# Rows of queries and keys with the heads next to each other, stacked by three DMAs of 256 KB for twelve of 64 KB

## The chip, the cores and the metric

The kernel runs on one core of a Trainium2 chip. The metric is the device time of one execution in microseconds. TensorE (PE) multiplies, VectorE (DVE), ScalarE (ACT) and GpSimd (POOL) work element by element, SyncE (SP) issues most DMAs. Each engine executes its own queue in order, and they meet at semaphores.

## The reference

Eight images of 512 tokens by 512 features go through an attention layer and a quantized feed-forward layer, each followed by an addition and a normalisation:

```python
q = (x @ Wq)  # 16 heads of 32;  k, v = x @ Wk, x @ Wv  # 4 heads, each for 4 query heads
attn = softmax(q k^T / sqrt(32));  x = layernorm(x + (attn v) @ Wo)
w_q = int8(round(weight / w_scale));  x_q = int8(round(x / x_scale))   # per row
x = layernorm(x + (x_q @ w_q^T) * x_scale * w_scale + bias)
```

## The kernel before

**Split numbers.** Matrix products are made from operands split in a high part (float32r) and a low part. A projection (`front_job`, L344, matmuls at L341) takes 12 matmuls of 128 x 512: four slices of the features, each high times high, high times low and low times high. Its result is 128 rows by 512 tokens: four heads of 32 rows, one below the other. ACT casts it to the high part (L657), DVE subtracts to get the low part (L843), into `q_parts` or `k_parts`.

**Stacks.** Scores use one matmul over 96 rows in place of three over 32: for a key head the rows are its 32 high, 32 low and 32 high rows, for the query the 32 high, high and low rows. So each head's rows have to be moved from where the projection put them to partitions 0 to 95. `stack_heads` (L307) does that with a DMA for each of 4 heads and 3 parts: 12 DMAs of 32 partitions x 2 KB. There are five such jobs per image: K, Q0, Q1, Q2 and Q3, where Qi holds the i-th query head of each of the four groups. SP issues them at L312; in the first image POOL issues those of Q0 and Q2. Two more rows of a stack (98 in all) hold the negative row maxima, high and low, sent by two small DMAs (`stack_max`, L1184, L1187) as soon as DVE has made the low part (L877).

**Units.** An image is 64 units: 4 query groups x 4 key tiles x 4 heads. In unit u TensorE makes one transposed score tile (`scores_t`, L416), which ACT exponentiates (L695), and one plain score tile (`scores`, L385) that lies 24 units ahead, of which DVE takes the row maxima (L865). Every 8 units come 2 steps of probabilities times values (L433). POOL adds the four key tiles of the probabilities (`add_probs`, L1080): 12 additions of 128 x 512 per group of 16 units. TensorE makes column sums of the result (`sums`, L459, into z_bank); the first additions of the next group wait for the evacuation of the sums before. ACT and DVE turn the sums into reciprocals.

**Plan.** All other work is laid into the units by dictionaries written in the code: `MIDDLE` (L49) for images 1 to 6, which do the projections of the image after and the tail of the image before beside their own attention, `FIRST` for image 0 and `LAST` for image 7. `sums_pe=(5, 18, 39, 54)` says at which units the column sums of the four groups before are issued. A place in the plan is the place in the engine's queue. If what it waits for is late, everything behind it on that engine is late.

**Tail.** A tile of 128 tokens goes through: output projection (`wo_pe`), residual and statistics on DVE (`res1`, `stats1`), inverse deviation on POOL (`rstd1`, `inv_std`, L1085 to L1090), normalisation on ACT (`norm1`, L723), maximum and scale on DVE (`maxx`, L927 to L933), rounding on ACT (`round`, L733, `unround`, L739), a DMA transpose on SP (`turn`, L1203), the integer product on TensorE (`ffn`, L529), and rescale, bias (POOL, L1098), residual, second statistics and second normalisation (`norm2`). SP also loads residual tiles (L1193), loads x (L1171) and stores results (L1197).

**Start.** Image 0 makes its first scores straight from the projections, four heads in separate row groups (L398), so its K and Q0 need the heads one below the other. The weights of Wk and Wv are cast at L676 and L851, those of Wq at L681 and L856.

Of the kernel before, what the change touches and what calls it, by code (L numbers as in the profile page):

```python
# [13 lines left out]
P = 128  # L14
# [35 lines left out]
    front_pe={Q3: (0, 1, 3, 4), 0: (5,), 1: (10,), 2: (13,), 3: (16,), K: (18, 22), Q0: (23, 24, 25, 27), V: (29, 30), VT: (33,), Q1: (36, 37), Q2: (44, 45)},  # L50
    front_act={Q3: 3, 0: 5, 1: 10, 2: 13, 3: 16, K: 22, Q0: 27, V: 29, VT: 32, Q1: 38, Q2: 45},
    front_dve={Q3: 4, 0: 6, 1: 11, 2: 15, 3: 16, K: 22, Q0: 27, Q1: 39, Q2: 45},
    sums_pe=(5, 18, 39, 54),
    inv_act=(6, 18, 39, 54),
    correct_dve=(7, 18, 40, 55),
    scale_dve=(7, 23, 40, 55),
    norm_dve=(9, 26, 45, 56),
    max_pe=(11, 25, 43, 57),
    max_hi_act=(10, 25, 43, 56),
    max_lo_dve=(11, 26, 45, 59),  # L60
    o_hi_act=(10, 29, 46, 57),
    o_lo_dve=(12, 29, 47, 63),
    wo_pe=((9, 11, 14), (19, 20, 21, 22), (31, 34), (39, 40, 42)),
    load_sp=(5, 17, 27, 39),
    res1_dve=(15, 22, 34, 42),
    stats1_dve=(17, 22, 34, 44),
# [9 lines left out]
    rescale_dve=(29, 36, 49, 57),  # L76
    res2_dve=(30, 36, 52, 60),
    stats2_dve=(33, 38, 52, 61),
# [20 lines left out]
    front_dve={Q3: 13},  # L99
    sums_pe=(6, 22, 37, 55),  # L100
    inv_act=(6, 22, 37, 55),
    correct_dve=(6, 23, 39, 53),
    scale_dve=(7, 23, 40, 54),
    norm_dve=(8, 23, 41, 58),
    max_pe=(13, 28, 43, 63),
    max_hi_act=(12, 27, 43, 61),
    max_lo_dve=(13, 27, 43, 59),
    o_hi_act=(9, 32, 42, 58),
    o_lo_dve=(12, 34, 42, 59),
    wo_pe=((10, 11, 13, 14), (20, 23, 25), (31, 33, 35, 36), (40, 44)),  # L110
    load_sp=(4, 18, 28, 42),
    res1_dve=(13, 25, 35, 43),
    stats1_dve=(15, 27, 36, 44),
    rstd1_pool=(18, 30, 41, 47),
    norm1_act=(18, 29, 38, 51),
    maxx_dve=(19, 30, 39, 48),
    round_act=(21, 31, 43, 53),
    unround_act=(24, 33, 45, 57),
    turn_sp=(26, 30, 46, 57),
    bias_pool=(21, 36, 52, 61),  # L120
    load_x_sp=(28, 35, 53, 59),
    ffn_pe=(28, 38, 53, 59),
    rescale_dve=(28, 38, 49, 60),
    res2_dve=(29, 38, 49, 61),
    stats2_dve=(29, 42, 49, 61),
    rstd2_pool=(32, 47, 57, 62),
    norm2_act=(35, 46, 59, 63))
# [8 lines left out]
WO_HI_ACT = (0, 1, 3, 5)  # L136
WO_LO_DVE = (0, 5, 7, 8)
# [18 lines left out]
def attention_ffn_kernel(nc, x, wq, wk, wv, wo, w_ffn, bias_ffn, out):  # L156
# [9 lines left out]
    STACKED = 16 * 3 * NKV  # L166
# [4 lines left out]
    with ExitStack() as ctx:  # L171
# [6 lines left out]
        def sem(name):  # L178
            return ctx.enter_context(nc.semaphore(name))
# [54 lines left out]

        wq_raw, wkv_raw, wo_raw = probs[:, 0], probs[:, 1], prob_sum[:]
# [6 lines left out]
        wkv_in = (sem("wk_in"), sem("wv_in"))  # L242
        wkv_hi_done, wkv_lo_done, wq_hi_done, wq_lo_done = (sem(n) for n in ("wkv_hi_done", "wkv_lo_done", "wq_hi_done", "wq_lo_done"))
# [85 lines left out]
        def _(pe):  # L329
# [14 lines left out]
            def front_job(b, f, to, v_parts, numbers=range(PASSES)):  # L344
# [7 lines left out]
                else:  # L352
# [10 lines left out]
            def front_in_turn(b, f, part, parts):  # L363
                if part == 0:
# [6 lines left out]
                    if isinstance(b, int) and b == 0:  # L371
                        pe.wait_ge(wq_lo_done, GROUPS)
# [904 lines left out]
```

## Time and profile before

| what | us |
|---|---|
| median of 3 runs | 787.58 |
| lowest and highest | 785.78, 792.46 |
| the profiled execution | 787.02 |
| its span | 785.2 |
| PE busy | 735.6 |
| POOL busy | 596.8 |
| DVE busy | 615.2 |
| ACT busy | 477.5 |

The profile is of one execution. Busy time is the time in which an engine executed an instruction; the mean granted TensorE clock was 0.985 of full speed. SP's queue is shown as SPq: the time there is that of issuing DMAs. "Idle before, releaser" is the time an engine stood still ahead of an instruction and what ended it. PEld is TensorE's weight load, which comes ahead of its matmul; a wait in front of a matmul shows there first.

### The profile page before, as it was taken

To read this page: it belongs to the slowest core of one execution; us is meant where nothing else is said; L and a number is where in the kernel's file an instruction comes from. 1 tells how busy PE (TensorE), PEld (TensorE's weight loads), DVE (VectorE), ACT (ScalarE), POOL (GpSimd) and SP (SyncE) were. 2 spreads that over 40 slices of the span, in tenths; PEclk is the share of its full clock that TensorE was granted. 3 is DMA by queue.
4 is the path that set the end of the run, shared out by engine and by line. 5 is a ranking of instruction groups with operands and counts; after the bars stand their busy time and mean duration, and the time that the engine had idled before them with its cause. 6 is when DMAs were issued, how large, how long until landed. Compare 5 with 4: busy or idle time off the path is not lost.

```text
span 785.2 us, 12326 instructions
## 1 busy us (share of the span) xinstructions
PE 735.6 (94%) x3700; PEld 433.8 (55%) x3700; DVE 615.2 (78%) x1090; ACT 477.5 (61%) x872; POOL 596.8 (76%) x705
## 2 busy tenths in 40 slices
PE   8789989899899999999999999999999999999993
PEld 6455545566366654566446663666545664454451
DVE  3797888668987788886888789878888868888546
ACT  3165556556765576656666566656756666666735
POOL 4258858676997689885987779975998759898935
PEclk9799999999999999999999999999999999999997
DMA  7632223133231342223322332413422233022121
GB/s 213 175 95 55 56 58 96 52 91 101 67 111 46 101 100 91 69 72 91 95 80 71 95 101 63 122 41 94 108 84 68 76 93 102 28 56 67 51 47 54
DMA packets 56386, 65.57 MB, mean 84 GB/s; under 512 B 25665, under 2 KB 27713, under 8 KB 56321
## 3 DMA queue, kind: packets, MB, share of 16 engines
q1 hardware_dynamic: 55152, 61.91, 29.5%
q0 software_dynamic: 1168, 2.89, 1.5%
q8 instruction: 30, 0.49, 0.3%
q14 instruction: 36, 0.29, 0.1%
HBM read 20.71 MB, written 8.39 MB: 37 GB/s over the span
## 4 chain that ended last, share of the span: by engine, by line
PE 45%; POOL 16%; issue 15%; SPq 10%; ACT 4%; DVE 4%; DMA 3%; POOLq 3%; DVEq 0%; ACTq 0%
POOL prob_sum L1080 14%; PE front_bank L341 9%; SPq L312 9%; PE st_bank L416 8%; PE s_bank L385 7%; PE o_bank L433 7%; PE tail_bank L341 6%; PE z_bank L459 3%; POOLq L1089 2%; DVE row_max L865 2%; ACT probs L695 1%; PE front_bank L348 1%; PE tail_bank L529 1%; DMA xq_sb<-round_sb 1%; POOL x_tok L1098 1%
## 5 line engine op out<-in xcount | busy, mean ns | idle before, releaser
L865 DVE TENSOR_REDUCE row_max<-s_bank 128x1 f32<-128x512 f32 x496 | 329.1, 682 | 81.2 <-PE s_bank L385 78.4
L695 ACT ACTIVATE probs<-st_bank 128x512 f32<-128x512 f32 x512 | 290.4, 594 | 133.1 <-PE st_bank L416 114.5
L1080 POOL TENSOR_TENSOR prob_sum<-prob_sum,probs 128x512 f32<-128x512 f32 x248 | 310.6, 1285 | 8.1 <-ACT probs L695 8.1
L416 PE MATMUL st_bank<-q_stack,k_stack 98*128 98x512 f32 x512 | 224.6, 441 | 14.6 <-ACT probs L695 11.1
L385 PE MATMUL s_bank<-k_stack,q_stack 96*128 96x512 f32 x496 | 203.4, 412 | 8.3 <-DVE row_max L865 7.1
L1080 POOL TENSOR_TENSOR prob_sum<-probs 128x512 f32<-128x512 f32 x128 | 161.3, 1284 | 46.0 <-PE z_bank L459 23.9
L416 PEld LDWEIGHTS st_bank<-q_stack,k_stack 98*128 98x128 f32 x512 | 96.1, 188 | 104.8 <-ACT probs L695 55.0
L433 PE MATMUL o_bank<-probs,v_tok 128*32 128x512 f32 x1024 | 123.3, 598 | 0.1
L385 PEld LDWEIGHTS s_bank<-k_stack,q_stack 96*128 96x128 f32 x496 | 94.2, 190 | 40.2 <-DVE row_max L865 22.5
L1085 POOL TENSOR_TENSOR rs<-mv,small 128x1 f32<-128x1 f32 x64 | 12.2, 190 | 82.1 <-DVE mv L915 81.5
L433 PEld LDWEIGHTS o_bank<-probs,v_tok 128*32 128x32 f32 x1024 | 26.7, 109 | 59.4 <-issue 52.5
L341 PE MATMUL front_bank<-x_hi,wq_hi 128*128 128x512 f32 x120 | 49.2, 410 | 0.0
L341 PE MATMUL tail_bank<-wo_hi,o_hi 128*128 128x512 f32 x116 | 47.7, 411 | 0.0
L341 PE MATMUL front_bank<-x_lo,wq_hi 128*128 128x512 f32 x120 | 47.7, 397 | 0.0
L341 PE MATMUL front_bank<-x_hi,wq_lo 128*128 128x512 f32 x120 | 47.4, 395 | 0.0
L341 PE MATMUL tail_bank<-wo_lo,o_hi 128*128 128x512 f32 x116 | 46.3, 399 | 0.0
L341 PE MATMUL tail_bank<-wo_hi,o_lo 128*128 128x512 f32 x116 | 46.2, 398 | 0.0
L1088 POOL TENSOR_TENSOR rs<-rs,small 128x1 f32<-128x1 f32 x64 | 35.1, 548 | 11.5 <-issue 2.5
L1098 POOL TENSOR_TENSOR x_tok<-x_tok,bias 128x512 f32<-128x512 f32 x28 | 36.1, 1289 | 1.3 <-ACT round_sb L733 1.3
L459 PE MATMUL z_bank<-prob_sum,ones 128*32 128x512 f32 x248 | 32.8, 600 | 2.5 <-POOL prob_sum L1080 2.4
L751 ACT ACTIVATE z_sb<-z_sb,rs 128x512 f32<-128x512 f32 x28 | 22.7, 812 | 16.8 <-POOL rs L1090 16.7
L701 ACT ACTIVATE inv_sum<-z_bank 128x512 f32<-128x512 f32 x32 | 19.2, 599 | 22.2 <-PE z_bank L459 22.1
(199 smaller groups left out, 992.8 us busy)
## 6 DMA issues: line engine op xcount, KB each, us to landing
q_stack<-q_parts SPq DMA_DIRECT2D x348, 64.0 KB, 2.0
x_tok<-in_L_attn_x SPq DMA_DIRECT2D x36, 256.0 KB, 3.0
y_sb<-in_L_attn_x SPq DMA_DIRECT2D x28, 256.0 KB, 2.8
out<-z_sb SPq DMA_DIRECT2D x28, 256.0 KB, 2.1
k_stack<-k_parts SPq DMA_DIRECT2D x84, 64.0 KB, 2.0
probs<-in_L_attn_Wq SPq DMA_DIRECT2D x1, 1024.0 KB, 7.6
prob_sum<-in_L_attn_Wo POOLq DMA_DIRECT2D x4, 256.0 KB, 4.3
q_stack<-neg_max SPq DMA_DIRECT2D x64, 8.0 KB, 1.8
```

What stands on the lines that cost most here:

```text
L312: eng.dma_start(dst[r * HEAD:(r + 1) * HEAD, j, :].bitcast(F32), part[j * HEAD:(j + 1) * HEAD, :]).then_inc(done, 16)
L341: last = nc.tensor.matmul(dst, left(c), right(c), start=(n == 0), stop=(n == PASSES - 1), skip_group_check=True)
L385: nc.tensor.matmul(s_bank[:, qt % 2, :], q_stack[0:STACK, i, j, qt * P:(qt + 1) * P], k_stack[0:STACK, p, j, :], start=True, stop=True).th ...
L416: nc.tensor.matmul(st_bank[:, j % 2, :], k_stack[0:STACK_M, p, j, kt * P:(kt + 1) * P], q_stack[0:STACK_M, i, j, :], start=True, stop=True ...
L433: last = nc.tensor.matmul(o_bank[rows, :], v_tok[:, p, kt, rows], probs[:, kt, j, :], start=(kt == 0), stop=(kt == QT - 1), skip_group_che ...
L459: last = nc.tensor.matmul(z_bank[j * HEAD:(j + 1) * HEAD, :], ones[:, 0:HEAD], prob_sum[:, j, :], start=True, stop=True, skip_group_check= ...
L695: nc.scalar.activation(probs[:, kt, j, :], st_bank[:, j % 2, :], ACT.Exp, scale=SCALE).then_inc(exp_done, 1)
L751: nc.scalar.activation(w["z"], w["z"], ACT.Identity, bias=rs2[:, t, 2:3], scale=rs2[:, t, 1:2]).then_inc(out_done, 1)
L865: nc.vector.tensor_reduce(row_max[:, i % 2, j * QT + qt:j * QT + qt + 1], s_bank[:, qt % 2, :], AX_X, ALU.max).then_inc(max_done, 1)
L1080: nc.gpsimd.tensor_tensor(prob_sum[:, j, :], first, probs[:, kt, j, :], ALU.add).then_inc(sum_done, 1)
L1088: nc.gpsimd.tensor_tensor(rs[:, t, 1:2], rs[:, t, 0:1], small[:, 0:1], ALU.pow)
L1098: nc.gpsimd.tensor_tensor(xn, xn, bias[:], ALU.add).then_inc(xb_done, 1)
```

## The change

The 128 rows that a projection makes are ordered by dimension first and head second (row 4d + j) in place of head first (row 32j + d). Then the four heads of one dimension lie in four neighbouring partitions, and a DMA that reads 128 partitions of 2 KB and writes 32 partitions of 4 x 2 KB moves all four heads of a part at once. A job is 3 DMAs of 256 KB.

The order comes from the columns of the weights. The casts of jobs 1 to 3 of Wq read the columns in the new order. K and Q0 of image 0 keep the old order and get their own weights in the space of `o_lo`; ACT lays them anew for images 1 to 7 with four copies in units 7, 9, 11 and 13 of image 0. The first K and Q0 are still stacked with `stack_heads`. The plans `MIDDLE` and `LAST` have new units for many entries; `FIRST` is unchanged.

```diff
+LAY_ACT = (7, 9, 11, 13)
-    STACKED = 16 * 3 * NKV
+    STACKED = 16 * 3
+        wk_first, wq_first = ([o_lo[:, n + h, :].rearrange("p (c n) -> p c n", c=KC) for h in range(2)] for n in (0, 2))
+        def stack_job(eng, dst, parts, done):
+            for r, part in enumerate(parts):
+                eng.dma_start(dst[r * HEAD:(r + 1) * HEAD, :, :].bitcast(F32), part).then_inc(done, 16)
...
+                    if b == 0 and f in (K, Q0):
+                        hi, lo = wk_first if f == K else wq_first
+                    if b == 1 and f in (K, Q0):
+                        pe.wait_ge(w_laid, 2 if f == K else 4)
...
 ACT, wq_part(i), i > 0 (DVE the same for wq_lo)
+                    nc.scalar.copy(wq_hi[:, :, i, :].rearrange("p c (d j) -> p c d j", j=NKV),
+                                   wq_raw.rearrange("p c (j i d) -> p i c d j", j=NKV, i=GROUPS)[:, i]).then_inc(wq_hi_done, 1)
+            def lay_weights(n):
+                if n == 0:
+                    act.wait_ge(wkv_lo_done, 1)
+                    act.wait_ge(wq_lo_done, 1)
+                source = (*wk_first, *wq_first)[n]
+                laid = (wkv_hi[:, :, 0, :], wkv_lo[:, :, 0, :], wq_hi[:, :, 0, :], wq_lo[:, :, 0, :])[n]
+                nc.scalar.copy(laid.rearrange("p c (d j) -> p c d j", j=NKV),
+                               source.bitcast(F32).rearrange("p c (j d) -> p c d j", j=NKV)).then_inc(w_laid, 1)
...
 DVE, o_split_lo
+                if n == 0:
+                    dve.wait_ge(w_laid, 4)
...
 POOL, Q2 of image 0
-            stack_heads(pool, range(NKV), q_stack[:, 2, :, :], (hi, hi, lo), first_q2_stacked)
+            stack_job(pool, q_stack[:, 2, :, :], (hi, hi, lo), first_q2_stacked)
...
 SP, every K and Q job but the first K and Q0
-                    stack_heads(sp, range(NKV), k_stack[:, p, :, :], (hi, lo, hi), k_stacked)
+                    stack_job(sp, k_stack[:, p, :, :], (hi, lo, hi), k_stacked)
-                    stack_heads(sp, range(NKV), q_stack[:, i, :, :], (hi, hi, lo), q_stacked[i])
+                    stack_job(sp, q_stack[:, i, :, :], (hi, hi, lo), q_stacked[i])
...
 MIDDLE (of the 30 entries, those that the prediction speaks of, and their neighbours)
-    max_lo_dve=(11, 26, 45, 59),
+    max_lo_dve=(11, 29, 44, 57),
-    norm1_act=(18, 27, 38, 47),
-    maxx_dve=(20, 28, 39, 47),
-    round_act=(21, 31, 39, 47),
-    unround_act=(22, 31, 43, 52),
-    turn_sp=(21, 29, 42, 49),
-    bias_pool=(26, 38, 44, 55),
-    load_x_sp=(1, 2, 3, 7),
-    ffn_pe=(27, 36, 48, 56),
+    norm1_act=(20, 26, 38, 47),
+    maxx_dve=(20, 29, 39, 47),
+    round_act=(21, 31, 40, 47),
+    unround_act=(22, 31, 42, 53),
+    turn_sp=(19, 31, 42, 47),
+    bias_pool=(25, 37, 43, 55),
+    load_x_sp=(1, 2, 2, 10),
+    ffn_pe=(28, 36, 49, 56),
```

## Rows read from the trace of the kernel before

Rows 2 and 3 are cut at the starts of the column sums (L459). Their columns are: the stretch, its length in us, busy us and instructions of PE, PEld, DVE, ACT and POOL, the granted clock, the share of the DMA engines, GB/s.

**Rows 1.** Busy time of each engine over the span, from the profile page.

```profile
PE 735.6 (94%) x3700; PEld 433.8 (55%) x3700; DVE 615.2 (78%) x1090; ACT 477.5 (61%) x872; POOL 596.8 (76%) x705
```

**Rows 2.** Windows view, units 18 to 39, six images: stretch, us, busy us, clock, DMA.

```profile
146.02:185.99 39.97, 37.80 (x185) 24.88 (x188) 28.86 (x54) 22.08 (x40) 22.14 (x33) 0.96 0.26 67
240.38:277.22 36.84, 36.05 (x184) 23.72 (x187) 28.65 (x54) 22.08 (x40) 22.11 (x32) 1.00 0.28 73
331.62:368.53 36.91, 36.10 (x184) 23.74 (x187) 28.65 (x54) 22.08 (x40) 22.13 (x32) 1.00 0.29 73
423.84:460.27 36.43, 36.25 (x185) 23.73 (x187) 28.80 (x54) 22.11 (x40) 22.35 (x33) 1.00 0.30 74
514.68:550.60 35.92, 35.92 (x185) 23.74 (x188) 28.67 (x54) 22.08 (x40) 22.12 (x33) 1.00 0.29 74
605.25:642.20 36.95, 36.13 (x184) 23.74 (x187) 28.66 (x54) 22.09 (x40) 22.13 (x32) 1.00 0.28 72
```

**Rows 3.** Windows view, units 39 to 54 of images 2 and 3, then 54 to 5.

```profile
277.22:296.18 18.96, 18.17 (x88) 10.64 (x81) 16.77 (x33) 13.69 (x26) 18.19 (x20) 1.00 0.47 112
368.53:388.10 19.57, 18.18 (x88) 10.54 (x80) 16.36 (x32) 13.68 (x26) 18.79 (x20) 1.00 0.43 108
296.18:315.27 19.09, 17.65 (x88) 8.91 (x89) 15.72 (x28) 11.33 (x22) 18.06 (x21) 1.00 0.26 84
```

**Rows 4.** Timeline of POOL: start us, duration us, what, count; eight additions.

```profile
321.42 9.97 POOL L1080 TENSOR_TENSOR prob_sum<-prob_sum,probs 128x512 f32<-128x512 f32 x8
```

**Rows 5.** Timeline of the SP queue, image 3: start us, duration us, what, count.

```profile
351.92 7.49 SPq L312 DMA_DIRECT2D q_stack<-q_parts  x12
359.52 1.94 SPq L1203 DMA_TRANSPOSE xq_sb<-round_sb  x1
...
379.68 1.22 SPq L1187 DMA_DIRECT2D q_stack<-neg_max  x2
```

**Rows 6.** Timelines of ACT, DVE and PE's weight loads: work before and after those DMAs.

```profile
355.08 0.63 ACT L739 ACTIVATE round_sb<-round_sb 128x512 bf16<-128x512 f32 x1
...
377.72 0.27 DVE L877 SCALAR_TENSOR_TENSOR neg_max<-o_bank,neg_max 16x128 fp32r<-16x128 f32 x1
...
363.05 0.55 PEld L529 LDWEIGHTS tail_bank<-w_int,xq_sb 128*128 128x128 bf16 x4 [1.23 <-DMA xq_sb<-round_sb]
...
382.20 0.19 PEld L416 LDWEIGHTS st_bank<-q_stack,k_stack 98*128 98x128 f32 x1 [1.86 <-DMA q_stack<-neg_max]
```

**Rows 7.** DMA issues by line: spread of issue times in ns; page: median us to landing.

```profile
L312 SPq DMA_DIRECT2D q_stack<-q_parts x348: 507/590/1857, 50.1 to 699.6; - x174
L1171 SPq DMA_DIRECT2D x_tok<-in_L_attn_x x32: 333/394/1498, 0.7 to 597.8; - x32
...
q_stack<-q_parts SPq DMA_DIRECT2D x348, 64.0 KB, 2.0
probs<-in_L_attn_Wq SPq DMA_DIRECT2D x1, 1024.0 KB, 7.6
```

**Rows 8.** Timelines of POOL, ACT and PE's weight loads: image 1 after unit 18.

```profile
150.90 0.56 POOL L1088 TENSOR_TENSOR rs<-rs,small 128x1 f32<-128x1 f32 x1 [2.54 <-issue]
...
151.84 0.81 ACT L723 ACTIVATE x_tok<-y_sb,rs 128x512 f32<-128x512 f32 x1 [3.36 <-POOL rs L1090]
...
153.18 0.19 PEld L416 LDWEIGHTS st_bank<-q_stack,k_stack 98*128 98x128 f32 x1 [2.61 <-ACT probs L695]
```

**Rows 9.** Timeline of PE's weight loads in the first image.

```profile
32.01 0.29 PEld L385 LDWEIGHTS s_bank<-k_stack,q_stack 96*128 96x128 f32 x1 [1.03 <-DMA q_stack<-probs]
61.65 0.19 PEld L416 LDWEIGHTS st_bank<-q_stack,k_stack 98*128 98x128 f32 x1 [1.55 <-DMA q_stack<-neg_max]
```

**Rows 10.** The casts of Wq and the widest reduction of DVE, by line (ns).

```profile
L681 ACT CAST wq_hi<-probs x4: 619/621/624, 10.8 to 20.2; 128x512 fp32r<-128x512 f32 x4
L856 DVE TENSOR_TENSOR wq_lo<-probs,wq_hi x4: 683/688/694, 11.4 to 37.0; 128x512 fp32r<-128x512 f32 x4
L872 DVE TENSOR_REDUCE row_max<-s_bank x4: 1217/1226/1229, 18.4 to 27.8; 128x2 f32<-128x1024 f32 x4
```

More of the change, by code:

```diff
@@ L98 @@
     front_act={Q3: 9},
-    front_dve={Q3: 13},
+    front_dve={Q3: 10},
     sums_pe=(6, 22, 37, 55),
     inv_act=(6, 22, 37, 55),
[L102 to L108, printed above, removed]
+    correct_dve=(6, 23, 38, 51),
+    scale_dve=(7, 23, 40, 53),
+    norm_dve=(8, 23, 42, 59),
+    max_pe=(13, 27, 42, 61),
+    max_hi_act=(12, 26, 43, 58),
+    max_lo_dve=(13, 28, 44, 59),
+    o_hi_act=(11, 34, 42, 58),
     o_lo_dve=(12, 34, 42, 59),
     wo_pe=((10, 11, 13, 14), (20, 23, 25), (31, 33, 35, 36), (40, 44)),
[L111 to L117, printed above, removed]
-    unround_act=(24, 33, 45, 57),
[L119 to L127, printed above, removed]
+    load_sp=(4, 19, 28, 41),
+    res1_dve=(13, 25, 35, 45),
+    stats1_dve=(14, 27, 37, 45),
+    rstd1_pool=(18, 30, 42, 47),
+    norm1_act=(18, 29, 39, 51),
+    maxx_dve=(19, 29, 39, 48),
+    round_act=(20, 31, 43, 53),
+    unround_act=(24, 33, 45, 57),
+    turn_sp=(23, 33, 45, 55),
+    bias_pool=(21, 36, 54, 59),
+    load_x_sp=(28, 36, 51, 63),
+    ffn_pe=(28, 38, 52, 59),
+    rescale_dve=(28, 38, 48, 61),
+    res2_dve=(29, 38, 49, 62),
+    stats2_dve=(29, 39, 49, 62),
+    rstd2_pool=(32, 45, 57, 61),
+    norm2_act=(35, 46, 58, 63))
 def plan_of(front, tail):
@@ L370, in front_in_turn @@
                         wait(pe, front_lo, b * SPLITS + (SPLIT_AT[Q0] + 1 if f == V else SPLIT_AT[f]))
-                    if isinstance(b, int) and b == 0:
+                    if b == 0:
                         pe.wait_ge(wq_lo_done, GROUPS)
+                    if b == 1 and f in (K, Q0):
+                        pe.wait_ge(w_laid, 2 if f == K else 4)
                 front_job(b, f, front_bank, k_parts, share(part, parts) if f >= K and f != VT else range(PASSES))
@@ L379, in scores @@
                     if b == 0 and i == 1:
-                        pe.wait_ge(first_k_stacked[j], STACKED // NKV)
+                        pe.wait_ge(first_k_stacked[j], STACKED)
                     if i == 0 and j == 0:
@@ L411, in scores_t @@
                 if u < NKV and b == 0:
-                    pe.wait_ge(first_k_stacked[j], STACKED // NKV)
-                    pe.wait_ge(first_q_stacked[j], STACKED // NKV)
+                    pe.wait_ge(first_k_stacked[j], STACKED)
+                    pe.wait_ge(first_q_stacked[j], STACKED)
                     pe.wait_ge(stack_ones, 1)
@@ L675, in wkv_part @@
                 act.wait_ge(wkv_in[n], 16)
-                nc.scalar.copy(wkv_hi[:, :, n, :], wkv_raw[:, :, n * P:(n + 1) * P]).then_inc(wkv_hi_done, 1)
+                nc.scalar.copy(wkv_hi[:, :, 1, :] if n else wk_first[0], wkv_raw[:, :, n * P:(n + 1) * P]).then_inc(wkv_hi_done, 1)
             def wq_part(i):
                 act.wait_ge(wq_in, 16)
-                nc.scalar.copy(wq_hi[:, :, i, :].rearrange("p c (j d) -> p c j d", j=NKV),
-                               wq_raw.rearrange("p c (j i d) -> p i c j d", j=NKV, i=GROUPS)[:, i]).then_inc(wq_hi_done, 1)
+                if i == 0:
+                    nc.scalar.copy(wq_first[0].rearrange("p c (j d) -> p c j d", j=NKV),
+                                   wq_raw.rearrange("p c (j i d) -> p i c j d", j=NKV, i=GROUPS)[:, 0]).then_inc(wq_hi_done, 1)
+                else:
+                    nc.scalar.copy(wq_hi[:, :, i, :].rearrange("p c (d j) -> p c d j", j=NKV),
[8 more added lines that the diff above has]
+                               source.bitcast(F32).rearrange("p c (j d) -> p c d j", j=NKV)).then_inc(w_laid, 1)
             def exp(b, u):
@@ L790, in segment @@
                                                  bias=-ROUND).then_inc(w_t_read, 1)
+                        if not tail and u == LAY_ACT[t]:
+                            lay_weights(t)
                         if not tail and u == WO_HI_ACT[t]:
@@ L1145, in _ @@
             for j in range(NKV):
-                pool.wait_ge(first_k_stacked[j], STACKED // NKV)
-                pool.wait_ge(first_q_stacked[j], STACKED // NKV)
+                pool.wait_ge(first_k_stacked[j], STACKED)
+                pool.wait_ge(first_q_stacked[j], STACKED)
             nc.gpsimd.memset(stack_mark[:, 0:1], 0.0).then_inc(k_stacked, STACKED)
```

52 lines of the change are left out of this document (30 added, 22 removed).

## The prediction

> **What bounds the kernel now.** The busy shares come first: TensorE is busy for 735.6 of 785.2 us and no other engine passes 78% [rows 1]. That share is a mean over stretches with different limits, so the second view cuts the steady images at the starts of the column sums (the z_bank matmuls, due at units 5, 18, 39 and 54 of the 64 units of an image). Six images can then be laid side by side, and two regimes show.
>
> From unit 18 to 39 TensorE is the limit. In image 5 it is busy for 35.92 of 35.92 us, POOL for 22.12 [rows 2]. From 39 through 54, 5 and on to 18 POOL sets the pace: it is busy for 18.19 of 18.96 us and 18.06 of 19.09 us [rows 3], because every group of 16 units needs 12 additions on POOL and eight of them take 9.97 us [rows 4], so twelve take 15.0 us, and biases and inverse deviations come on top. In these stretches TensorE has under a microsecond of slack, and a short wait of TensorE is mostly made up while POOL goes on.
>
> The third view is SP's queue. Stacking one job occupies it for 7.49 us, twelve issues of 590 ns at the median [rows 5, 7]. What is queued behind is late. In image 3 the rounding of a tile ended at 355.71 us (355.08 plus 0.63), but its DMA transpose was issued at 359.52 us, when the stack was through, and TensorE then lost 1.23 us on it [rows 5, 6]. Later the low part of the maxima was ready at 377.99 us, its DMA went out at 379.68 us, and TensorE waited 1.86 us [rows 5, 6]. So the twelve DMAs themselves are rarely waited for. The small transfers behind them are.
>
> **The change part by part.**
>
> *Twelve issues become three.* The trace has no 256 KB copy inside SBUF. Its issue is bounded by the 64 KB one (590 ns) and by the load of 256 KB into 128 partitions (394 ns) [rows 7]. I take 0.5 us, the middle: 1.5 us of queue per job for 7.5, 6.0 us less, 36 times from SP (7 K jobs, 29 Q jobs) and once for the first Q1. When the last byte lands is bounded from below by the 64 KB landing of 2.0 us after the third issue, 1.0 + 2.0 = 3.0 us after the first, and from above by the 1 MB load, 7.6 us for more bytes than the 768 KB of a job [rows 7]; the old form needs 11 x 0.59 + 2.0 = 8.5 us. I take 5 us. The old scores tolerate 8.5 us, so the stacks themselves gain nothing on the path.
>
> *Steady images, units 18 to 39.* Image 5 has no such wait and takes 35.92 us; images 2, 3, 4 and 6 take 36.84, 36.91, 36.43 and 36.95 [rows 2]. The excess is 0.92 + 0.99 + 0.51 + 1.03 = 3.45 us, and the 1.23 us wait for the transpose [rows 6] is about its size. With the queue free 6 us earlier the transpose goes out when the rounding ends. I take all 3.45 us. The bounds are 0 (another wait fills the gap) and 3.45: TensorE can't do better than no idle time.
>
> *Units 39 to 54.* Image 3, with the late maxima, takes 19.57 us, image 2 takes 18.96 [rows 3]. The 1.86 us wait costs 0.61 us, since POOL is the limit. Two images are like this: 1.2 us. The same DMA waits in the other images cost nothing here, and their removal gains nothing.
>
> *Image 1.* Its stretch takes 39.97 us, 4.05 us over image 5 [rows 2]. POOL sat idle for 2.54 us inside its first inverse deviation, waiting for nothing that the profile shows; ACT, in order, waited 3.36 us at its first normalisation, with the exponentials queued behind it, and TensorE lost 2.61 us [rows 8]. The granted clock of the stretch is 0.96, where all others have 1.00 [rows 2]: after that idle time TensorE ran a while at the lower of its two levels (1.2 GHz for 2.4), which makes up the remaining 1.4 us. The change does not touch POOL, but its plan moves this normalisation from unit 18 to 20, so that two more exponentials stand ahead of it. A unit of this stretch is 35.92 / 21 = 1.71 us [rows 2], and two give TensorE 3.4 us of work, more than the 2.61 us. I take 4.1 us; the ends are 0 and 4.1.
>
> *First image.* A score waited 1.03 us for the stack of Q1 and a later one 1.55 us for the maxima behind the stack of Q3 [rows 9]. The first becomes a wait for the transposed maxima, which came just before it: 0.7 us. Of the second only the queue's part goes, and I take half, 0.8 us. Together 1.5 us, between 0 and 2.6.
>
> *Casts with heads innermost.* Jobs 1 to 3 of Wq are now read with steps of 128 elements and written in sequence, on ACT (0.62 us each) and DVE (0.69 us each) [rows 10]. No row has such a step. The lower end is the same instruction with runs of 32 elements, no change; the upper end is two elements' time for one, as in the reduction of 1024 elements that takes 1.23 us [rows 10], so 0.6 us more on ACT and 0.7 us on DVE, three times. DVE works without a break over most of that time, so its part could land in full: 3 x 0.7 = 2.1 us, and 0.6 us for the ACT cast that Q1 waits for, 2.7 us. I take 0, by the nearest row, and keep 2.7 for the range.
>
> The SBUF page of the Trainium skill ("SBUF — State Buffer", Specifications) says that fewer than two hits on each 16-byte line cost bandwidth, which speaks against this part: each of these reads would open a new line. It gives no figure for an engine, and no row here shows it. By that rule the sum would hold up to 2.7 us more.
>
> *Four new copies on ACT* (the weights of K and Q0 laid anew, units 7, 9, 11, 13 of the first image): 4 x 0.62 = 2.5 us by the casts [rows 10]. Image 0 is where ACT has most room. I take a quarter on the path, 0.6 us, between 0 and 2.5 (5.0 with the doubled read). The new waits on these copies come more than ten units later and cost nothing. The Q2 stack on POOL, three issues for twelve, frees POOL while it waits for other things: nothing.
>
> *The other shifts of the plan,* one to three units either way, move no matmul across units 5, 18, 39 or 54 and no work of POOL between the stretches. I price them at zero.
>
> **The sum.** 3.45 + 1.2 + 4.1 + 1.5 - 0.6 = 9.65 us. The profiled execution took 787.02 us for its span of 785.2 us; 787.02 - 9.65 = 777.4 us. It lies 0.56 us under the median of 787.58 us, so on the median's scale 777.9, rounded to 778 us.
>
> **Rivals.**
>
> *The gain is hidden or refilled.* The queue was late mostly in stretches where POOL sets the pace, and ACT or DVE may fill the 0.9 us per image between 18 and 39. Then only the first-image terms and some of the rest remain, 2 to 5 us: 783 to 786 us. For it: four fifths of the removed queue time is in no wait of TensorE. Against it: image 5 shows the pace without the wait under the same load. Chance 0.27.
>
> *The strided casts and copies cost.* 2.7 us for the casts and up to 4.4 us more for the copies take 3 to 7 us from the gain: 781 to 785 us. This is what the skill's rule on lines would do here. Chance 0.10.
>
> *Slower: the normalisation now stands too close to its rounding.* In every tail image the plan puts the first normalisation on ACT at unit 20, the maximum of that tile on DVE at 20 and the rounding on ACT at 21. Before, three exponentials lay between; now one does. The maximum takes a reduction and two small operations, 1.1 us or so (0.7 us as for a DVE pass [rows 10] and two short ones), with a row maximum of 0.7 us perhaps ahead, and ACT covers 0.6 us of it. A wait of 0.5 to 1.2 us follows on ACT, with the exponentials behind it, in the stretch where TensorE has no slack. Seven times up to 1.2 us is 8.4 us, which leaves the gain near zero; if it also brings the lower clock, as in image 1, up to 1.4 us more each time, 18 us in all: 778 + 18 = 796 us. It decides the sign from about 1.4 us per image (9.65 / 7). Two exponentials' distance in a queue with 40% idle time speaks against it. Chance 0.08, 788 to 796 us.
>
> *The wide DMA doesn't do what it says.* If its descriptors go out slower than four of 64 KB do, the burst lands after more than 8.5 us and scores wait. The 1 MB load (7.6 us) speaks against it. Chance 0.03, above 790 us.
>
> **How the numbers follow.** The forecast (774 to 780.5 us) has 0.48; more than that (POOL's stretches shorten too, or the first image gains more) has 0.04, under 774 us. A measurement of this kernel tells about 1% (7.9 us) from no change: faster means under 779.7 us, slower over 795.5 us. Of the forecast 0.44 lies under the first bound, with the 0.04 and 0.02 of the strided case 0.50. Slower has 0.05 (the upper half of the last two cases). Same has 0.45. The range runs from 772 us, below which 0.03 is left, to 788 us, above which about 0.11 is left.
>
> **What would show it.** Right: SP's stack of a job takes under 2 us of queue; TensorE's wait for the transposed tile is gone or under 0.3 us; all stretches from unit 18 to 39 take 35.9 to 36.2 us; image 1 has clock 1.00 there; the POOL-bound stretches keep 18.96 and 19.1 us. Wrong: an ACT wait for the scale of x of over 1 us per image, casts of Wq of 1.2 us, or stretches from 18 to 39 that keep 36.9 us with another releaser. The forecast falls if the stretch of image 5 is not the floor for the others, or if image 1's idle POOL still reaches TensorE.

## The result: slower by 1.65%

| | before | changed |
|---|---|---|
| median, us | 789.04 (4 runs) | 802.23 (4 runs) |
| lowest and highest, us | 785.78, 792.46 | 798.98, 804.93 |
| span of the profiled execution, us | 785.2 | 799.7 |

The ratio of changed to before is 1.0165, with a 95% interval of 1.0133 to 1.0198. The forecast of 778 us (772 to 788) and the expected sign were both wrong. The interval lies wholly above 1, though the change is smaller than 2%.

The profile after shows first what the change did to the queues. From the page of the changed kernel, the DMA queue, the issues by line (count, KB each, median us to landing), and the spread of issues by SP in the timeline of image 3:

```profile
q1 hardware_dynamic: 49824, 61.89, 42.1%
...
q_stack<-q_parts SPq DMA_DIRECT2D x87, 256.0 KB, 5.6
k_stack<-k_parts SPq DMA_DIRECT2D x21, 256.0 KB, 5.6
```

```profile
354.08 1.85 SPq L321 DMA_DIRECT2D q_stack<-q_parts  x3
355.98 0.60 SPq L1230 DMA_DIRECT2D y_sb<-in_L_attn_x  x1
356.62 1.22 SPq L1224 DMA_DIRECT2D q_stack<-neg_max  x2
360.17 1.23 SPq L1240 DMA_TRANSPOSE xq_sb<-round_sb  x1
```

A job takes 1.85 us of SP's queue for 7.49 us [rows 5]. The forecast was 1.5 us, and under 2 us as a sign that it was right. But each wide DMA lands 5.6 us after its issue, where a 64 KB one took 2.0 us [rows 7]. The hardware queue moved about the same bytes (61.89 MB; 61.91 before), and its packets took 42.1% of the DMA engines' time where the profile page of before had 29.5%.

Now the same cuts at the column sums. Units 18 to 39 of the six middle images, then 39 to 54 and 54 to 5 of images 2 and 3, and units 6 to 22 of the last image, whose plan has its first sums there (the changed kernel, windows view, columns as in [rows 2]):

```profile
149.85:189.81 39.96, 37.88 (x184) 24.83 (x187) 29.69 (x55) 22.48 (x40) 22.09 (x33) 0.96 0.41 67
244.09:282.31 38.22, 36.30 (x184) 23.67 (x187) 29.48 (x55) 22.23 (x40) 22.09 (x33) 1.00 0.42 70
336.56:374.95 38.39, 36.22 (x184) 23.66 (x187) 29.45 (x55) 22.22 (x40) 22.06 (x33) 1.00 0.43 69
429.25:469.16 39.91, 37.87 (x185) 24.81 (x188) 29.66 (x55) 22.25 (x40) 22.16 (x33) 0.96 0.41 67
523.42:561.73 38.31, 36.22 (x184) 23.66 (x187) 29.45 (x55) 22.22 (x40) 22.07 (x33) 1.00 0.42 70
615.99:654.27 38.28, 36.24 (x184) 23.66 (x187) 29.44 (x55) 22.23 (x40) 22.06 (x33) 1.00 0.42 70
sum 233.07, PE 220.73 PEld 144.29 DVE 177.17 ACT 133.63 POOL 132.53; mean PE 36.79 PEld 24.05 DVE 29.53 ACT 22.27 POOL 22.09
...
282.31:301.15 18.84, 18.24 (x87) 10.70 (x80) 16.96 (x33) 13.69 (x26) 18.14 (x20) 1.00 0.83 120
301.15:320.24 19.09, 17.86 (x88) 9.04 (x89) 15.64 (x28) 12.03 (x23) 18.09 (x21) 1.00 0.24 78
692.20:714.65 22.45, 19.40 (x92) 11.33 (x92) 15.27 (x28) 12.34 (x24) 17.09 (x17) 0.92 0.30 48
```

The six TensorE-bound stretches take 233.07 us, where those of [rows 2] add up to 223.02. The POOL-bound ones keep their length: 18.84 and 19.09 us for 18.96 and 19.09 [rows 3]. Units 6 to 22 of the last image take 22.45 us and took 18.33 us before. What fills the difference stands in the waits of TensorE's weight loads, in images 3 and 7 (timeline of the changed kernel):

```profile
363.79 0.19 PEld L429 LDWEIGHTS st_bank<-q_stack,k_stack 98*128 98x128 f32 x1 [2.62 <-DMA q_stack<-neg_max]
...
708.19 0.19 PEld L429 LDWEIGHTS st_bank<-q_stack,k_stack 98*128 98x128 f32 x1 [3.91 <-DMA q_stack<-neg_max]
```

In each of images 1 to 6 the transposed score of unit 32 waits 2.4 to 2.6 us for the maxima of its group; in image 7 one waits 3.91 us. In image 3 the small DMAs went out at 356.62 us, behind the stack of Q0. The DMA view of just this window gives the time to their landing (changed kernel, `--dma --window 356.5:358`):

```profile
q_stack<-neg_max SPq DMA_DIRECT2D x2, 8.0 KB, 6.7
```

Over the whole kernel the median of these DMAs is 1.9 us. With that, the second one, issued at about 357.2 us, would have landed near 359.1 us, and the load could have started without a wait at 363.79 - 2.62 = 361.17 us. So it is not the late unit alone that makes TensorE wait. In image 7 it is the stack of Q3 that stands ahead: it goes out at 699.66 us and the small DMAs at 702.58 us, while the kernel with two entries back sends the first of them ahead of that stack.

Where did the 14.5 us of span go? Up to the first column sum of image 0 (70.47 us before, 75.42 after) 5.0 are lost. The six stretches lose 10.05. The last image, from the sum at unit 54 of the one before to the end, loses 3.1 (123.5 us before, 126.6 after). The rest of image 0 gains 1.1 and the other stretches of images 1 to 6 gain 2.5: 5.0 + 10.05 + 3.1 - 1.1 - 2.5 = 14.5 us. The parts in image 0 are of one trace each and are not steady: of the nine experiments below with the full kernel seven take 77 us for the rest of image 0, with a stretch at the lower clock in it, and two 74.4 us, as the changed kernel does; before takes 75.6 us.

The loss in the first image has its own rows. The casts of Wq and the four new copies in the changed kernel (by line; count, duration in ns as min/median/max, start):

```profile
L698 ACT CAST wq_hi<-probs x3: 1085/1127/1128, 13.8 to 20.7; 128x512 fp32r<-128x512 f32 x3
...
L891 DVE TENSOR_TENSOR wq_lo<-probs,wq_hi x3: 1032/1059/1077, 14.9 to 37.8; 128x512 fp32r<-128x512 f32 x3
...
L708 ACT CAST wkv_hi<-o_lo x1: 1094/1094/1094, 53.8 to 53.8; 128x512 fp32r<-128x512 f32 x1
```

Against 0.62 and 0.69 us in [rows 10] these are 1.13 and 1.06 us, and a copy takes 1.1 us.

### The profile page after: what moved, and what is told of

Read it like the earlier page. It is cut to its first block, busy times and chain, and to the rows that moved or that the text cites. A ratio compares the mean times of both kernels' runs of the same rounds, so it can differ in the third digit from the quotient of the medians.

```text
span 799.7 us, 11986 instructions
## 1 busy us (share of the span) xinstructions
PE 742.5 (93%) x3700; PEld 439.8 (55%) x3700; DVE 616.9 (77%) x1090; ACT 485.2 (61%) x876; POOL 592.3 (74%) x696
## 3 DMA queue, kind: packets, MB, share of 16 engines
q1 hardware_dynamic: 49824, 61.89, 42.1%
## 4 chain that ended last, share of the span: by engine, by line
PE 54%; POOL 15%; issue 13%; DVE 5%; ACT 5%; DMA 4%; SPq 2%; POOLq 2%; DVEq 0%; ACTq 0%
POOL prob_sum L1117 13%; PE front_bank L349 11%; PE st_bank L429 9%; PE tail_bank L349 9%; PE s_bank L398 8%; PE o_bank L446 8%; DMA q_stack<-neg_max 4%; PE z_bank L472 4%; ACT probs L722 2%; PE front_bank L356 2%; POOLq L1126 1%; SPq L321 1%; DVE row_max L900 1%; DVE row_max L907 1%; POOL probs L1135 1%
## 5 line engine op out<-in xcount | busy, mean ns | idle before, releaser
L398 PE MATMUL s_bank<-k_stack,q_stack 96*128 96x512 f32 x496 | 205.6, 416 | 4.7 <-DVE row_max L900 4.3
L472 PE MATMUL z_bank<-prob_sum,ones 128*32 128x512 f32 x248 | 32.8, 600 | 2.9 <-POOL prob_sum L1117 2.8
L920 DVE SCALAR_TENSOR_TENSOR z_bank<-z_bank,inv_sum 128x512 f32<-128x512 f32 x32 | 22.3, 697 | 16.8 <-ACT inv_sum L730 16.7
```

Of the source, the lines that this page charges most:

```text
L398: nc.tensor.matmul(s_bank[:, qt % 2, :], q_stack[0:STACK, i, j, qt * P:(qt + 1) * P], k_stack[0:STACK, p, j, :], start=True, stop=True).th ...
L472: last = nc.tensor.matmul(z_bank[j * HEAD:(j + 1) * HEAD, :], ones[:, 0:HEAD], prob_sum[:, j, :], start=True, stop=True, skip_group_check= ...
L920: nc.vector.scalar_tensor_tensor(out=z_bank, in0=z_bank, scalar=-1.0, in1=inv_sum[:], op0=ALU.mult, op1=ALU.mult).then_inc(correct_done, 1)
```

## The experiments

Theory A: the loss behind the first image comes from the place of the maxima's small DMAs behind a wide stack. Two plan entries put them there. Its rival B: the wide DMAs or the layout cost in every image. Each ratio below is to the kernel before as measured beside that experiment, with a median between 788.9 and 790.2 us.

**The new layout with the old plans.**

```diff
-    (the changed MIDDLE and LAST)
+    (MIDDLE and LAST of the kernel before, word for word)
```

> The changed kernel with the plans of the kernel before (MIDDLE and LAST); layout, copies and wide DMAs stay. Theory A (the maxima's DMAs stand behind the wide stack of Q0, put there by the plan's unit 29 for 26, and of Q3 in the last image, 10 for 13, and the stack takes the DMA engines some 7 us): TensorE's wait for neg_max at unit 32 is gone, the stretch from unit 18 to 39 takes 35.9 to 36.9 us for 38.3, and only the 3.8 us of the first image (strided casts and copies) stand against the gain of the free queue: 785 to 790 us, ratio to before 0.995 to 1.003. Theory B (the layout and the wide DMAs cost by themselves in every image): ratio above 1.01.

Measured: 788.72 us, ratio 0.9987 (0.9964 to 1.0010), inside A's range. The stretches take 35.92 to 36.17 us in images 2 to 6 and 38.04 us in image 1; the first column sum starts at 75.1 us. The wide DMAs are the same as in the changed kernel, so B falls. The change without its new plans costs in the first image and gains in the others, and the two cancel.

**The new plans with only two entries put back.**

```diff
-    max_lo_dve=(11, 29, 44, 57),      # MIDDLE
+    max_lo_dve=(11, 26, 44, 57),
-    front_dve={Q3: 10},               # LAST
+    front_dve={Q3: 13},
```

> The changed kernel with two entries of its plans put back: the low part of the maxima of the third group at unit 26 for 29 in the middle images, and the low part of Q3 at unit 13 for 10 in the last. Theory A: these two carry the loss behind the first image; 802.2 falls by 10 to 13 us to 789 to 792 us, ratio 1.000 to 1.006, and the wait for neg_max falls from 18.9 us to under 4 us in total. Theory B: under 3 us are won, ratio 1.013 or more.

Measured: 783.85 us, ratio 0.9905 (0.9874 to 0.9936), even 5 us better than A expected. Of the 18.9 us in which weight loads waited for neg_max, 0.8 us are left, in the last image, and none at unit 32. The six stretches take 36.11, 36.01, 35.96, 36.05, 36.04 and 35.97 us. That of image 1, in the windows view of this kernel:

```profile
151.65:187.76 36.11, 36.11 (x187) 23.71 (x191) 29.49 (x55) 22.11 (x40) 22.16 (x33) 1.00 0.45 75
```

TensorE is busy in all of it, at full clock. Two numbers out of some sixty entries turn this change from 1.65% slower to 1% faster.

**The old layout with the new plans.**

```diff
-    (MIDDLE and LAST of the kernel before)
+    (those of the changed kernel, word for word)
```

> The kernel before with the plans of the changed one: twelve DMAs of 64 KB, old layout. Theory A says that the order matters and that the old form suffers more from it: the stack holds SP's queue for 7.5 us, the maxima land about 1.5 us later than behind the wide one, a wait of 3.5 to 4.5 us in each of 7 images: 802 to 815 us, ratio 1.02 to 1.035. Theory B (the loss is the wide DMA's): ratio under 1.005.

Measured: 828.99 us, ratio 1.0483 (1.0445 to 1.0521), more than the upper end. The stretches from unit 18 to 39 take 41.7 to 44.1 us. The waits of weight loads for neg_max, by total us, number and longest:

```profile
PEld st_bank L416 <- DMA q_stack<-neg_max: 45.2, 17, 5.6
```

So the new order is harmful with either form of stack, and more so with the old one. There the wait is SP's queue: in image 3 the stack of Q0 holds it from 360.21 us for 8.25 us, the small DMAs go out at 369.14 us and land 2.3 us later. With the wide form they go out sooner and land late (6.7 us). The mean granted clock fell to 0.958. So the wide DMA did not make the order harmful, it made the harm smaller.

**DMAs alone.** A kernel that only moves tiles inside SBUF, four times each; attention is left out and the output is a copy of x. Its core:

```diff
+ heads: eng.dma_start(dst[32*r:32*(r+1), j, :], source[32*j:32*(j+1), part, :])   # 12 times
+ jobs:  eng.dma_start(dst[32*r:32*(r+1), :, :], source[:, part, :])               # 3 times
+ flats: eng.dma_start(dst[:, r, :], source[:, part, :])                           # 3 times
+ ...max: the same, and behind it two of 8 KB into row 96 and 97
```

> Only DMAs inside SBUF from SP's queue, each set alone, waited for before the next, four times; no attention is computed, the output is a copy of x. Sets: one of 64 KB (32 to 32 partitions), twelve of them, one of 256 KB (128 to 32 partitions), three of them, three of 256 KB from 128 to 128 partitions, six of 128 KB (64 to 16 partitions), and the two small ones alone, behind twelve, behind three, and from ACT's queue beside three. If the writes into 32 partitions are what is slow, three wide ones take 6 to 7 us, three flat ones under 4.5 us, and twelve of 64 KB are bound by their issue (about 8.5 us). If the DMA engines' rings are first in, first out, the small ones behind the wide ones land 5 to 7 us after the first issue, and from ACT's queue earlier; alone they take 2 us. If the wide DMA has no price of its own, three take 4 us and the small ones behind them 2.5 us.

Measured, as issues by line (count, KB each, median us to landing) and then as SP's queue, where each set starts when the one before has landed:

```profile
d_heads<-source SPq DMA_DIRECT2D x48, 64.0 KB, 2.0
...
d_jobs<-source SPq DMA_DIRECT2D x12, 256.0 KB, 5.6
...
d_flats<-source SPq DMA_DIRECT2D x12, 256.0 KB, 2.4
...
d_headsmax<-small SPq DMA_DIRECT2D x8, 8.0 KB, 1.8
d_jobsmax<-small SPq DMA_DIRECT2D x8, 8.0 KB, 6.0
d_jobsact<-small ACTq DMA_DIRECT2D x8, 8.0 KB, 5.9
```

```profile
4.21 7.48 SPq L32 DMA_DIRECT2D d_heads<-source  x12
13.10 7.47 SPq L32 DMA_DIRECT2D d_headsmax<-source  x12
...
27.20 1.88 SPq L37 DMA_DIRECT2D d_jobs<-source  x3
35.26 1.85 SPq L37 DMA_DIRECT2D d_jobsmax<-source  x3
```

Twelve narrow ones take 8.9 us from first issue to landing (4.21 to 13.10), three wide ones 8.1 us (27.20 to 35.26), more than the 6 to 7 us expected. So a stack is hardly ready sooner than before. What the change saves is queue, and what was a row of issues is now a backlog in the DMA engines: a small DMA behind the twelve lands in 1.8 us, behind the three in 6.0 us. From ACT's queue, issued 1.35 us after the first wide one, it takes 5.9 us, so it is not the order in SP's queue alone that holds it back; the expectation that another queue would help failed. Three flat DMAs of the same size need 3.7 us in this trace, and the small ones behind them land after 2.0 us (the row below), so the backlog is not one of bytes: it comes with the slow shape.

```profile
d_flat<-small SPq DMA_DIRECT2D x8, 8.0 KB, 2.0
```

Six DMAs of 128 KB (64 to 16 partitions) move the same job in 8.4 us, so splitting it does not help.

**Shapes of the wide DMA.** The same kind of kernel, with only DMAs between sets of partitions.

```diff
+ rows:   dst[0:32, :, :]    <- spare[0:32, :, :]      # 256 KB, 32 to 32 partitions
+ wide:   dst[:, 0, :]       <- spare[0:32, :, 0:512]  # 256 KB, 32 to 128
+ spread: dst[0:64, 0:2, :]  <- source[:, 0, :]        # 256 KB, 128 to 64
```

> Only DMAs inside SBUF again, each set alone: 256 KB from 128 to 32 partitions (4.0 us alone, three 8.1 us in the run before), 256 KB from 32 to 32 partitions with the same rows of 2 KB times four, 256 KB from 32 to 128, 256 KB from 128 to 64, 64 KB from 128 to 32 in pieces of 512 B, and 64 KB from 32 to 32. If the number of partitions written sets the time, 32 to 32 takes 4 us as well, 32 to 128 takes 2.5 us and 128 to 64 about 3 us or, if 64 partitions are no better than 32, 4 us. If the mismatch of the two sides is what costs, 32 to 32 takes 2.5 us.

Measured, medians of four, columns as above:

```profile
d_jobs<-source SPq DMA_DIRECT2D x12, 256.0 KB, 5.6
d_rowss<-spare SPq DMA_DIRECT2D x12, 256.0 KB, 3.8
d_job<-source SPq DMA_DIRECT2D x4, 256.0 KB, 3.9
d_rows<-spare SPq DMA_DIRECT2D x4, 256.0 KB, 3.0
d_wide<-spare SPq DMA_DIRECT2D x4, 256.0 KB, 3.6
d_spread<-source SPq DMA_DIRECT2D x4, 256.0 KB, 3.9
```

Neither answer fits alone. With 32 partitions on both sides it takes 3.0 us, with 128 on both 2.3 us (the run before), with 128 on one side and fewer on the other 3.6 to 3.9 us. But the sets differ in their packets too. The DMA view of one repetition counts them, for 128 to 32 and then for 32 to 32 (`--window 4:8`, `16:19`):

```profile
DMA packets 144, 0.26 MB, mean 66 GB/s; under 512 B 16, under 2 KB 16, under 8 KB 144
DMA packets 48, 0.26 MB, mean 87 GB/s; under 512 B 16, under 2 KB 16, under 8 KB 16
```

The 32 to 32 set went in pieces of 8 KB, not of the 2 KB that the expectation names; all others went in 144 packets, the flat one too. So at equal packets, fewer than 128 partitions on one side cost 1.3 to 1.7 us (2.3 against 3.6 to 4.0 us). What part of the distance from 3.0 to 3.9 us is the mismatch of the sides and what part the number of packets is not separated.

**Where the step lies.** Theory A has a sharp edge: before or behind the stack of Q0, which stands at unit 27. Its rival E is gradual: the later the maxima, the longer the wait.

```diff
-    max_lo_dve=(11, 26, 44, 57),
+    max_lo_dve=(11, 27, 44, 57),      # in the other kernel 28
```

> The kernel with the two plan entries put back, but the low part of the maxima of the third group at unit 27. That is one unit later than 26, and still ahead of the stack of Q0 (unit 27) in SP's queue. Theory A (what counts is the place before or behind the stack): the stretches from unit 18 to 39 stay at 36.0 us and no wait for neg_max over 0.3 us appears at unit 32, median 782 to 786 us. Theory E (what counts is how late the maxima are made): the stretches grow by 0.5 to 1 us.

> The same with unit 28, the first place behind the stack of Q0. Theory A: the small DMAs are issued some 2 us earlier than with 29 at most, but land when the stack has landed, at about the same time as with 29: a wait of 2 to 2.6 us at unit 32 in six images, stretches of 38 us or so, median 794 to 798 us. Theory E: a third of the way from 26 to 29 is left, a wait of 0.8 to 1.7 us, median 788 to 792 us.

Measured: with 27, 784.11 us, ratio 0.9932 (0.9910 to 0.9954), stretches of 35.98 to 36.12 us and no wait for neg_max at unit 32 (two of 0.8 us stand elsewhere). In image 3 the small DMAs land after 2.1 us. With 28, 792.25 us, ratio 1.0029 (1.0001 to 1.0056), stretches of 37.25 to 37.82 us. With 29 they were 38.2 to 39.9 us. The edge is where A puts it, and E's growth of 0.5 to 1 us at 27 is not there. Behind the edge it is gradual too: waits of 1.3 to 2.0 us and the median lie nearer to what E expected for 28 than to A's numbers. SP's queue and a weight load of image 3 with 28:

```profile
352.87 1.85 SPq L321 DMA_DIRECT2D q_stack<-q_parts  x3
354.77 1.24 SPq L1224 DMA_DIRECT2D q_stack<-neg_max  x2
```

```profile
362.00 0.19 PEld L429 LDWEIGHTS st_bank<-q_stack,k_stack 98*128 98x128 f32 x1 [1.97 <-DMA q_stack<-neg_max]
```

Counted from the column sum at unit 18 of the image, the stack stands at 17.52 us in both traces, the small DMAs went out 0.64 us sooner than with 29 (the load of `y_sb` no longer stands between), took over 6 us to land in both, and the weight load started 0.58 us sooner. That is what the stretch of image 3 gains (37.82 us for 38.39). A's claim that 28 and 29 land at about the same time was too strong. In the profiled executions the six stretches take 224.7 us for 233.07; 3.2 us of the 8.4 are the lower clock of images 1 and 4, which no image has with 28.

**Only the middle images.**

```diff
-    max_lo_dve=(11, 29, 44, 57),      # MIDDLE; LAST keeps Q3 at 10
+    max_lo_dve=(11, 26, 44, 57),
```

> The changed kernel with only the entry of the middle images put back (26 for 29), the low part of Q3 in the last image stays at unit 10. Theory A: the six middle images are as in the kernel with two entries, the last image keeps its wait of 3.9 us, and the median lies 3 to 4.5 us above 783.9 us: 787 to 788.5 us, ratio 0.994 to 0.998.

Measured: 788.29 us, ratio 0.9985 (0.9965 to 1.0005); the time is as expected, the ratio just above. The last image keeps its wait of 3.9 us. So the entry of the middle images is worth 13.9 us (802.23 to 788.29) and that of the last 4.4 us (788.29 to 783.85), to about 1 us, since the kernels were not all measured beside each other; the kernel with unit 27, measured beside this one, gives 4.2 us for the last image. In the two profiled executions the six stretches differ by more, 233.07 against 216.12 us; 2.7 us of it come back in image 0, where of the two only this one has a stretch at the lower clock (units 11 to 23, 27.3 us at 0.94 for 24.6 at 1.00). Why is open.

**The first image: casts and copies in sequence.** From here on the base is the kernel with two entries put back. Theory C: the steps in reading cost. Theory D: the copies on ACT cost because they exist.

```diff
-  wq_hi[:, :, i, :].rearrange("p c (d j) -> p c d j", j=NKV), wq_raw.rearrange("p c (j i d) -> p i c d j", ...)[:, i]
+  wq_hi[:, :, i, :].rearrange("p c (j d) -> p c j d", j=NKV), wq_raw.rearrange("p c (j i d) -> p i c j d", ...)[:, i]
-  laid.rearrange("p c (d j) -> p c d j", j=NKV), source.bitcast(F32).rearrange("p c (j d) -> p c d j", j=NKV)
+  laid, source.bitcast(F32)
   (DVE's casts of Wq likewise)
```

> The kernel with the two plan entries put back, and all casts and copies of weights in the old order of columns, so read and written in sequence (the order of the heads in the weights is left out, the output is not the reference's). Theory C (steps in the reading cost in the first image): the casts of Wq fall from 1.1 to 0.62 us on ACT and 0.69 on DVE, the four copies from 1.1 to 0.6 us, and the sum at unit 5 of the first image starts 3 to 4 us earlier than the 77.2 us of the reordering kernel: span 776 to 777.5 us, ratio 0.985 to 0.988. Theory D (the first image is late because the copies exist at all, and the steps don't matter): under 1.5 us are won.

Measured: 779.75 us, ratio 0.9881 (0.9832 to 0.9930). Casts take 0.62 and 0.68 us, copies 0.60 to 0.63 us. The first column sum starts at 71.6 us for 77.2. But 77.2 is the latest of the seven traces with slow copies on ACT; the others have 74.8 to 75.8 us, so 3 to 5.5 us are won here. The span of 779.1 us misses the 776 to 777.5 expected.

**The loops turned, so that the writing has the steps.**

```diff
-  laid.rearrange("p c (d j) -> p c d j", j=NKV), source.bitcast(F32).rearrange("p c (j d) -> p c d j", j=NKV)
+  laid.rearrange("p c (d j) -> p c j d", j=NKV), source.bitcast(F32).rearrange("p c (j d) -> p c j d", j=NKV)
   (the casts of Wq likewise)
```

> The same kernel with the right order, but the loops of the casts and copies turned: the source is read in runs of 32 elements and the destination written in steps of 4 elements (16 bytes). If reading in steps is what costs and writing in steps is free, the ACT casts and copies take 0.62 us again and the span is that of the kernel in sequence, 776 to 777.5 us; if a step costs on either side, the casts keep 1.1 us and the span stays at 780 us.

Measured: 783.58 us, ratio 0.9923 (0.9896 to 0.9949); casts 1.11 us on ACT, 1.08 us on DVE, copies 1.11 to 1.13 us. A step costs the same on the side that writes.

**The copies on POOL.**

```diff
-                        if not tail and u == LAY_ACT[t]:
-                            lay_weights(t)                    # ACT
+            for n in range(4):
+                lay_weights(n)                                # POOL, behind the stacking of Q0
```

> The kernel with the two plan entries put back, and the four copies of weights taken from ACT (units 7 to 13 of the first image) to POOL, which waits some 17 us for Q2 before the first image. Theory D: ACT's 4.4 us of copies delay exponentials of the first image by about 3 us; without them the sum at unit 5 starts near 74 us for 77.2, span 776.5 to 778 us, ratio 0.986 to 0.989. Theory C: only the casts matter, under 1 us is won.

Measured: 779.14 us, ratio 0.9871 (0.9828 to 0.9915). This is the lowest median of all kernels, 23 us under the changed one and faster than the one before. A copy takes 1.05 to 1.08 us on POOL, in time in which it had nothing else to do. The first column sum starts at 70.5 us (74 expected), as before the change, though the casts still take 1.1 us.

Both ways of making ACT's copies cheap win 3.8 to 4.7 us, against the kernel with two entries back and against the turned loops, which were measured beside them. From the first transposed score to the first column sum it takes 33.5 us in the kernel before, 36.9 us in the changed one, 38.2 us with two entries back, 33.8 us in sequence and 32.8 us with the copies on POOL; all seven traces with slow copies on ACT have 36.7 to 38.3 us. Each of the seven, and none of the others, has a part at the lower clock there. A weight load behind the first copies and two windows of the kernel with two entries back, and two windows of the one with the copies on POOL:

```profile
55.83 0.19 PEld L429 LDWEIGHTS st_bank<-q_stack,k_stack 98*128 98x128 f32 x1 [1.38 <-ACT probs L722]
...
36.00:56.00 20.00, 17.59 (x74) 12.45 (x73) 16.95 (x29) 10.95 (x20) 2.78 (x8) 0.96 0.70 155
56.00:77.00 21.00, 19.48 (x84) 10.76 (x88) 11.48 (x19) 13.28 (x24) 14.57 (x12) 0.76 0.19 30
```

```profile
35.00:54.00 19.00, 17.58 (x74) 12.44 (x73) 16.22 (x28) 10.18 (x19) 2.50 (x7) 0.96 0.72 158
54.00:70.50 16.50, 15.50 (x84) 9.05 (x86) 12.06 (x21) 10.39 (x21) 14.94 (x12) 1.00 0.27 45
```

TensorE idled for the exponentials behind the copies, and then ran at the lower level for much of a stretch whose mean is 0.76. D is right that ACT is the wrong place and C that the step is the price: copies of 0.6 us on ACT take 1 us more than copies on POOL in that stretch (33.8 for 32.8 us). What the casts alone cost at the start is not settled. The first transposed score starts at 36.98 us before, 38.52 after, 37.73 with slow casts and copies on POOL, and 37.80 with fast casts; but the seven kernels that run the same start, up to the side of the step, have it anywhere from 36.6 to 38.9 us.

## Why the prediction was wrong

**The step that failed.** "*The other shifts of the plan* [...] I price them at zero." One of them, 26 to 29 for the maxima, was in the quoted diff. It moves no matmul over a cut and no work of POOL, which was the test applied, but it moves two small DMAs over the stack of Q0 in SP's queue. The prediction had found itself what is waited for ("The small transfers behind them are."), and yet did not ask which transfers the new plan puts behind. In their place the small DMAs land after 6.7 us in image 3, and TensorE waits 2.4 to 2.6 us in each middle image. It costs 13.9 us in the middle images, and its twin in the plan of the last image (10 for 13, outside the quoted diff) 4.4 us.

**The burst.** "I take 5 us" for the landing of a stack, with ends of 3.0 and 7.6. It is 8.1 us alone. The upper end came from a load from memory whose shape was another. The rival "the wide DMA doesn't do what it says" named the place, but had 0.03, and asked only whether the scores wait for the stack; they don't. The wait is of what lies behind it, at the engines in place of the queue. Its range, above 790 us, holds the measured time all the same, without its mechanism.

**Units 18 to 39: right in size.** The forecast took 35.92 us as floor for all. With the two entries back the stretches take 35.96 to 36.11 us, and with all of the old plans images 2 to 6 take 35.92 to 36.17 us, so the new plans are not needed for it.

**Image 1: right.** The 4.05 us over the floor were forecast to go with the normalisation at unit 20. With the new plans they are gone: 36.11 us at clock 1.00 with the two entries back, and with the old plans (normalisation at 18) 38.04 us. The normalisation was not moved by itself, so that it is this entry is argued, and half of the 4.05 us goes with the old plans too. In the changed kernel POOL's idle time is still there, 1.80 us:

```profile
154.14 0.57 POOL L1125 TENSOR_TENSOR rs<-rs,small 128x1 f32<-128x1 f32 x1 [1.80 <-issue]
```

but the 39.96 us of its image 1 are the new wait and the low clock (0.96) behind it.

**Units 39 to 54: right.** 1.2 us were forecast for the two images with late maxima. They take 18.84 us in the changed kernel for 19.57 and 19.50 us, 1.4 us less.

**POOL-bound stretches: right.** In the middle images they keep 18.8 to 19.4 us under every edit, with one exception (21.5 us at clock 0.84, with the old layout and the new plans). The prediction gives TensorE under a microsecond of slack in them; from 54 to 5 its own row has 19.09 - 17.65 = 1.44 us.

**First image: not separated.** 1.5 us were forecast. Both waits are gone from the changed kernel, but the casts and copies move the same start. With the copies on POOL the first column sum starts at 70.5 us, as before, so the net of what is left is near zero.

**The copies: too small.** 0.6 us was taken, bounds 0 to 5.0. They cost 4.7 us (783.85 to 779.14 when they move to POOL; 4.4 us against the turned loops, measured beside). TensorE waits longer for exponentials, and every trace with slow copies on ACT has a stretch at the lower clock that the others lack; I had not counted that such a wait can be paid twice. How much is due to each is not separated.

**The casts: the wrong end.** "I take 0, by the nearest row." A cast takes 1.8 times as long on ACT and 1.5 times on DVE: 512 elements with steps of 128 elements cost 0.5 and 0.4 us more, and so do the turned loops, with steps of 16 bytes in writing. What these microseconds cost the kernel is not settled, as said above. The rule of the Trainium skill on lines ("SBUF — State Buffer", Specifications) pointed this way, and the runs agree that one element per 16-byte line costs. No run has two elements on a line, so where the cost ends is not shown.

**The slower rival: not seen.** The rounding's wait for the scale of x grew only from 10.9 us in total, 13 times, to 14.1 us, 15 times, at most 1.3 us, and the stretches of 36.0 us show that TensorE doesn't feel it. The sign named for it, over 1 us per image, was there before the change too (10.9 us in 7 images) and so could not tell.

With the two entries put back the kernel takes 783.9 us, and 779.1 us with the copies on POOL as well, against the 778 us that the sum gave. The terms outside the failed steps held for units 18 to 54: with two entries back the six stretches from 18 to 39 take 216.1 us for 223.0, 6.9 of the 7.55 us forecast. That the last number comes within 1 us of 778 is in part luck, since the casts and copies were mis-sized and the kernel before, measured again, lies at 789 to 790 us and not at the 787.58 that the sum started from.

## What to carry to other kernels

When DMAs are merged, list what follows each of them in its queue and who waits for that. Fewer issues free the queue, but if the merged DMA is slow by its shape, as the one from 128 to 32 partitions here, the backlog stands in the DMA engines instead, and a small urgent transfer behind it lands late (6.0 us for 1.8), from another queue too (5.9 us). Behind three DMAs of the same size from 128 to 128 partitions it landed after 2.0 us: measure the shape alone first. Read each changed number of a written plan as a swap in some queue; the two that counted here were of three units each.

## What the runs showed of the hardware

- Copies of 256 KB inside SBUF, each alone, land after 2.3 us (128 to 128 partitions), 3.0 us (32 to 32), 3.6 us (32 to 128) and 3.9 to 4.0 us (128 to 32, 128 to 64). The 32 to 32 one went in 48 packets, the others in 144. Three of 128 to 32 in a row take 8.1 us, three of 32 to 32 5.6 us, three flat ones 3.7 us.
- Two DMAs of 8 KB land 1.8 us after issue alone or behind twelve DMAs of 64 KB, 2.0 us behind three flat ones of 256 KB, 6.0 us behind three of 256 KB from 128 to 32, and 5.9 us from ACT's queue beside them. In image 3 of the kernels they took 2.3 us behind a stack of twelve, 6.4 and 6.7 us behind a wide one.
- SP takes 0.6 us per issue, whether for 64 KB or for 256 KB inside SBUF.
- 512 elements of 4 bytes with a step of 16 bytes or more take 1.1 us on ACT for 0.62, 1.06 us on DVE for 0.69, and 1.06 us on POOL (no run has POOL's copy in sequence).
- A wait of TensorE of some 2.5 us is in some images followed by a stretch at the lower clock and in others not: images 1 and 4 of the changed kernel have 0.96 and lose 1.6 us more than the rest, with the same wait. At this place, none of the six waits of 1.3 to 2.0 us (unit 28) and all six of 4.3 to 5.6 us (old layout, new plans) came with a stretch below 1.00.
